# Three maxima and an all-partition reduction moved from the start of layer 1 to the end of layer 0, and two stores exchanged

## Chip, cores and metric

One core of one Trainium2 chip. The metric is the device time of one execution in microseconds (us). Of the kernel before there are three runs, and a profile of one further execution.

## The reference

Two graph-attention layers over the same 8192 nodes with 256 features; `adj` is a symmetric 0/1 matrix with about eight neighbours and the node itself in each row.

```python
h = maximum(layernorm(x), 0)                       # layer 0
Wh = h @ W
e  = (Wh @ a[:256])[:, None] + (Wh @ a[256:])[None, :]
x  = x + leaky_relu(softmax(where(adj == 0, -1e9, e)) @ Wh, 0.2)

h = maximum(layernorm(x), 0)                       # layer 1
h1, h2 = h @ a[:256], h @ a[256:]
e  = leaky_relu(h1 + h2.T, 0.01)
x  = x + softmax(where(adj > 0, e, -9e15)) @ h
```

## The kernel before, in words

Nodes are handled in T = 64 tiles of 128 rows. **Layer 0** is the first `nc.Block()`. For each tile the adjacency rows are loaded, converted, folded into 16-bit words and turned; TensorE multiplies the masks into the 64 value tiles (`aggregate`, L1016). VectorE (DVE) and ScalarE (ACT) then make the tile's new x (`normalise`, `add_x`, `copy_sums`), its new h (`finish`, L539), and the two products h1 and h2 (`dots`, L751), which `keep_dots` (L714 to L716) copies into `h1all`, `h2all` and the last column of `hh`; its three copies each raise `h12_kept`. SyncE (SP) stores x (`store_x1`, L372) and h (`store_h`, L377). The 46 tiles that come first also get a list of neighbours of each row; their rows are sorted by length, and the sorted records are written to memory by GpSimd (POOL), and loaded again by SP into `rec` (L400, semaphore `rec_in`).

At the end of layer 0 TensorE turns `h1all` (L1052), DVE copies the result out of PSUM (`h1T`, L968), and SP stores it as the h1 row (L404). SP then stores the last tile of h, and waits until all of its stores have landed (L405 to L412). The block's end is a barrier: no engine starts layer 1 before all have ended layer 0.

```python
sp.wait_ge(h1T_sb, 1)                               # L403
sp.dma_start(h1_d, h1T).then_inc(h1_out, 16)
store_h(T - 1, DENSE, NX - 1)
```

**Layer 1** is the second block, with two kinds of work side by side. The 18 remaining tiles are dense: TensorE multiplies masks (`adjp`, `adjn`) into two value arrays `Vp` and `Vn` (L1746), which are made in the first of six groups from tiles `hs` of h that SP loads; ACT makes the high halves (L1358) and DVE the low ones (L1521). The 46 sorted tiles are sparse: POOL gathers a row of h for each neighbour by indirect DMA (`gat`, L1334, 393 of them), ACT makes weights (L1390, L1398), DVE adds weighted rows (`sacc`, L1614 to L1636), and POOL scatters the 46 results (L1325). The gathers are made in batches of five or six rows with four buffers: before a batch is gathered, POOL waits until all rows of the batch four before it, whose buffer it takes, have been added (L1332, `row_added`); the first four batches hold 5, 6, 6 and 6 gathers, and the five batches behind them 5, 5, 5, 4 and 5; after the ninth (47 gathers) POOL scatters the first finished tile, and so on. SP holds six tiles' x for this work (L1229), and the load of the seventh waits for that first scatter; it stands in SP's program among the loads of `hs` (L1267), and those behind it wait with it. ACT and DVE issue dense and sparse work in an order written out by hand (`rows_by`, `prepare`, `add_rows`).

Before any of this, layer 1 takes the largest h2 of all nodes (it shifts the exponents), and two flags that say whether a list overflowed. DVE makes three maxima along the free axis into `red_in` (L1469, L1470, L1472; `exc` is L1468), POOL takes them over all partitions (L1321), and DVE goes on with `red` at L1476. POOL's first gather stands behind L1321 in its program, without needing its result:

```python
pool.wait_ge(mx_ready, 1)
nc.gpsimd.partition_all_reduce(red[:, :], red_in[:, :], P, RMAX).then_inc(M_all, 1)
```

SP begins layer 1 with loads: the h1 row to all partitions (L1212), four tiles of h (L1218), words of the adjacency (L1207), four more tiles (L1221).

Of the kernel before, what the change touches and what calls it, by code (L numbers as in the profile page):

```python
# [35 lines left out]
def two_layer_graph_attention(nc, x, adj, w0, a0, a1, key_pos, ident, tri, caps, row_ids, self_pos, out):  # L36
# [30 lines left out]
    P = 128  # L67
# [69 lines left out]
    with outer:  # L137
# [7 lines left out]
        cnt = outer.enter_context(nc.sbuf_tensor("cnt", [P, NS], f32))  # L145
        full = outer.enter_context(nc.sbuf_tensor("full", [P, 4], f32))
        idf = outer.enter_context(nc.sbuf_tensor("idf", [P, P], f32))


        ctx = ExitStack()  # L150
        with ctx:
            def sb(name, shape, dt):
                return ctx.enter_context(nc.sbuf_tensor(name, shape, dt))

            def sem(name):
                return ctx.enter_context(nc.semaphore(name))
# [145 lines left out]
            rank_ready = sem("rank_ready")  # L302
            rec_copied = sem("rec_copied")
            rec_in = sem("rec_in")
            h1T_ps = sem("h1T_ps")
            h1T_sb = sem("h1T_sb")
            h1_out = sem("h1_out")
# [17 lines left out]
            def _(sp):  # L325
# [49 lines left out]
                def store_h(t, off, b):  # L375
                    sp.wait_ge(h12_kept, 3 * t + 3)
                    sp.dma_start(h_rows(t + off), hh[:, b, :]).then_inc(hh_out[b], 16)  # L377

                def whole(t):

                    if t < T:
                        load(t, offset(t), range(0, 1), t == 0)
                    if PKL <= t < T + PKL:
                        store_words(t - PKL, offset(t - PKL), (t - PKL) % NPK)
                    if t < T:
                        load(t, offset(t), range(1, 2), t == 0)
                    if LAG <= t:
                        store_x1(t - LAG, offset(t - LAG), (t - LAG) % NX)
                    if XL <= t < T + XL:
                        load_x(t - XL, offset(t - XL), (t - XL) % NX, t - XL < NX)  # L390
                    if LAG + 1 <= t:
                        store_h(t - LAG - 1, offset(t - LAG - 1), (t - LAG - 1) % NX)
                    if t < T:
                        load(t, offset(t), range(2, Q), t == 0)
# [5 lines left out]
                sp.dma_start(rec_f[:, :, :], rec_d[:, 0:REC].rearrange("(m p) c -> p m c", p=P)).then_inc(rec_in, 16)  # L400
                for t in range(T + XL, T + LAG):
                    whole(t)
                sp.wait_ge(h1T_sb, 1)  # L403
                sp.dma_start(h1_d, h1T).then_inc(h1_out, 16)  # L404
                store_h(T - 1, DENSE, NX - 1)  # L405
                sp.wait_ge(rec_in, 16)
                sp.wait_ge(h1_out, 16)
                for b in range(NPK):
# [5 lines left out]
            @block.gpsimd  # L414
            def _(pool):

                nc.gpsimd.memset(eps[:, :], EPS).then_inc(ones_set, 1)
                nc.gpsimd.memset(hh[0:1, 0, 0:DV], 0.0).then_inc(dummy_set, 1)
                nc.gpsimd.memset(hh[0:1, 0, DV:ROW], NOTHING).then_inc(dummy_set, 1)
                nc.gpsimd.memset(HV[:, SH:T + SH, D:ROW], 1.0).then_inc(ones_set, 1)  # L420
                pool.wait_ge(dummy_out, 16)
                nc.gpsimd.memset(hh[:, :, D:DV], 1.0).then_inc(hh_ones, 1)
                pool.wait_ge(rmax_ready, 1)
                nc.gpsimd.partition_all_reduce(Mb[:, :], rmax[:, :], P, RMAX).then_inc(M_ready, 1)
                pool.wait_ge(rank_ready, 1)

                def copy_record(m):
                    nc.gpsimd.tensor_copy(xr[:, m % SH, 0:REC], rec_f[:, m, :]).then_inc(rec_copied, 1)

                def order(m):  # L430
                    pool.wait_ge(xs_in[m % SH], 16 * (m // SH + 1))
                    pool.wait_ge(rec_copied, m + 1)
                    pool.indirect_dma_start(rec_d, bass.IndirectOffsetOnAxis(ap=rank[:, m:m + 1], axis=0),
                                            xr[:, m % SH, :], None).then_inc(xs_out[m % SH], 16)

                for m in range(NS):
                    if m >= SH:
                        pool.wait_ge(xs_out[m % SH], 16 * (m // SH))
                    pool.wait_ge(x1_out[m % NX], 16 * (m // NX + 1))
                    pool.dma_start(xr[:, m % SH, REC:REC + D], x1_d[SP0 + m, :, :]).then_inc(xs_in[m % SH], 16)  # L440
                    copy_record(m)
                    if m >= 2:
                        order(m - 2)
                order(NS - 2)
                order(NS - 1)
                for i in range(SH):
                    pool.wait_ge(xs_out[i], 16 * len(range(i, NS, SH)))

            @block.scalar
            def _(act):  # L450
# [138 lines left out]
            def _(dve):  # L589
# [117 lines left out]
                def normalise(t, b):  # L707

                    dve.wait_ge(acc_ready, t + 1)
                    nc.vector.reciprocal(rden[:, b:b + 1], acc[b][:, D:DV]).then_inc(rden_ready, 1)  # L710

                def keep_dots(t, off, b):

                    nc.vector.tensor_copy(h1all[:, bass.ds(t + off, 1)], h12[:, 0:1]).then_inc(h12_kept, 1)  # L714
                    nc.vector.tensor_copy(h2all[:, bass.ds(t + off, 1)], h12[:, 1:2]).then_inc(h12_kept, 1)
                    nc.vector.tensor_copy(hh[:, b, DV:ROW], h12[:, 1:2]).then_inc(h12_kept, 1)  # L716
# [236 lines left out]
                for t in range(1, T):  # L953
                    step(t, t % UN, *counts(t), ahead=t + 1 < T, folds=t + 2 < T, listed=t + 2 < NS,
                         taken=t + 1 < NS, e=(t - 2) // UN if 2 <= t < NS + 2 else None)
                    if t == SORT:
                        sort_totals()
                    if t == SORT + 1:
                        sort_scan()
                    if t == SORT + 2:  # L960
                        sort_ranks()
                normalise(T - 1, 1)
                add_x(T - 1, NX - 1, *counts(T))
                scale_h(T - 1)
                dots(T - 1, NX - 1, counts(T)[2])
                keep_dots(T - 1, DENSE, NX - 1)
                dve.wait_ge(h1T_ps, 1)
                nc.vector.tensor_copy(h1T, kps[1][0:T, 0:P]).then_inc(h1T_sb, 1)  # L968

# [137 lines left out]
        with ctx:  # L1107
# [22 lines left out]
            tM = early[:, 6 * T:7 * T]  # L1130
            sS = early[:, 9 * T:9 * T + 2 * NS].rearrange("p (s t) -> p s t", s=2)
            tS = early[:, 11 * T:11 * T + NS]
            exc = sb("exc", [P, NS], f32)
            gat = sb("gat", [P, NBUF, BS, ROW], f32)
            sacc = sb("sacc", [P, NACC, 2, DV], f32)
            zself = sb("zself", [P, 2, NS], f32)
# [4 lines left out]
            hb = sb("hb", [P, 2, NS], f32)  # L1141
            srd = sb("srd", [P, 2], f32)
            M1 = sb("M1", [P, 4], f32)
            red_in = sb("red_in", [P, 3], f32)
            red = sb("red", [P, 3], f32)
            flag = sb("flag", [P, 1], f32)
            redi = sb("redi", [P, 1], i32)
            Es = sb("Es", [P, 2, T], f32)
# [8 lines left out]
            pkg_in = [sem(f"pkg_in{i}") for i in range(2)]  # L1157
            h1bc_in = [sem(f"h1bc_in{i}") for i in range(2)]
            x1g_in = sem("x1g_in")
            exc_ready = sem("exc_ready")  # L1160
            mx_ready = sem("mx_ready")
            M_all = sem("M_all")
            flag_ready = sem("flag_ready")
            redi_ready = sem("redi_ready")
            nh2_ready = sem("nh2_ready")
# [151 lines left out]

            @block.gpsimd
            def _(pool):
                pool.wait_ge(mx_ready, 1)  # L1320
                nc.gpsimd.partition_all_reduce(red[:, :], red_in[:, :], P, RMAX).then_inc(M_all, 1)  # L1321

                def scatter(m):
                    pool.wait_ge(so_ready, m + 1)
                    pool.indirect_dma_start(  # L1325
                        out, bass.IndirectOffsetOnAxis(ap=rec[:, m, OWN:OWN + 1], axis=0),
                        sout[:, m % NOUT, :], None).then_inc(so_out[m % NOUT], 16)

                done = 0
                for k, (m, s0, s1) in enumerate(batch):  # L1330
                    if k >= NBUF:
                        pool.wait_ge(row_added, begin[k - NBUF + 1])  # L1332
                    for s in range(s0, s1):
                        pool.indirect_dma_start(  # L1334
                            gat[:, k % NBUF, s - s0, :], None, h_d,
                            bass.IndirectOffsetOnAxis(ap=rec[:, m, s:s + 1], axis=0))\
                            .then_inc(gat_in[k % NBUF], 16)
                    while done < NS and last[done] + OUT_LAG <= k:
                        scatter(done)
                        done += 1  # L1340
                for m in range(done, NS):
                    scatter(m)
# [122 lines left out]
            def _(dve):  # L1465
                nc.vector.tensor_scalar(nh2[:, :], h2all[:, :], -BIG, None, ALU.mult)\
                    .then_inc(nh2_ready, 1)
                nc.vector.tensor_tensor(exc[:, :], rec_f[:, :, DEG], capv[:, :], ALU.subtract).then_inc(exc_ready, 1)  # L1468
                nc.vector.reduce_max(red_in[:, 0:1], h2all[:, :], AX.X)  # L1469
                nc.vector.reduce_max(red_in[:, 1:2], full[:, :], AX.X)  # L1470
                dve.wait_ge(exc_ready, 1)
                nc.vector.reduce_max(red_in[:, 2:3], exc[:, :], AX.X).then_inc(mx_ready, 1)  # L1472
                dve.wait_ge(M_all, 1)

                Mh = red[:, 0:1]
                nc.vector.tensor_scalar(M1[:, 2:3], Mh, -1.0, None, ALU.mult).then_inc(negM_ready, 1)  # L1476
# [319 lines left out]
```

## Time and profile before

| | |
|---|---|
| median of three runs | 1690.48 us |
| the three runs | 1688.31, 1690.48, 1691.74 us |
| the profiled execution | 1689.47 us |
| span from its first to its last instruction | 1687.3 us |
| mean granted TensorE clock | 0.973 |
| busy shares | PE 92%, DVE 74%, ACT 59%, POOL 33% |
| layer 1 | from 1069.1 us of the span to its end |

The profiled execution's own time is 2.2 us above its span; times in views are counted from the span's start. Busy shares average over two layers with different limits, so the views to read here are those of a stretch.

### The profile page before, as it was taken

How to read it: one execution, taken by the hardware profiler on the slowest of the kernel's cores; microseconds unless marked ns; L12 is line 12 of the kernel's file. 1: busy time of each engine (PE TensorE's matmuls, PEld its weight loads, DVE VectorE, ACT ScalarE, POOL GpSimd, SP SyncE). 2: the span in 40 equal slices, each digit the busy share in tenths (PEclk: the TensorE clock that was granted, in tenths of full speed). 3: DMA queues.
4: the chain of work that ended last, by engine and by line, in shares of the span. 5: the costliest groups of instructions: out<-in, count | busy, mean ns of one | idle time of the engine just before them, and what ended most of it. 6: DMA issues, size and time to landing. Idle time of an engine off the chain costs nothing. (4 is left out here: it accounts for less than half of the span.)

```text
span 1687.3 us, 37172 instructions
## 1 busy us (share of the span) xinstructions
PE 1551.5 (92%) x13443; PEld 1321.8 (78%) x13443; DVE 1255.9 (74%) x4759; ACT 989.5 (59%) x1514; POOL 562.5 (33%) x588
## 2 busy tenths in 40 slices
PE   6877999999999999999999999486898999989897
PEld 5645888888888888888888888365687877878786
DVE  6577998998898899887874453696866666666765
ACT  5978656665765566566666661675645445444542
POOL 0000000000000000000014554587777777777776
PEclk9998999999999999999999999798899999999999
DMA  9418989888988898898889994555444444444443
GB/s 318 172 43 341 348 303 364 320 301 313 369 310 300 329 358 310 301 374 319 331 337 385 393 361 112 178 132 153 119 135 114 130 123 129 115 142 117 128 113 107
DMA packets 141700, 406.91 MB, mean 241 GB/s; under 512 B 25857, under 2 KB 91586, under 8 KB 108834
## 3 DMA queue, kind: packets, MB, share of 16 engines
q1 hardware_dynamic: 116114, 335.11, 54.0%
q0 software_dynamic: 25488, 70.77, 14.7%
q8 instruction: 28, 0.46, 0.1%
q14 instruction: 70, 0.57, 0.1%
HBM read 365.39 MB, written 40.41 MB: 241 GB/s over the span
## 5 line engine op out<-in xcount | busy, mean ns | idle before, releaser
L1016 PE MATMUL banks<-HV,adjT 128*128 128x257 f16 x8192 | 938.8, 274 | 18.0 <-DVE adjT L673 10.2
L1016 PEld LDWEIGHTS banks<-HV,adjT 128*128 128x128 fp8e4 x8192 | 791.2, 97 | 150.8 <-DVE HV L703 23.8
L1746 PE MATMUL banks<-Vp,adjp 128*128 128x257 f16 x2304 | 451.9, 278 | 77.5 <-DVE adjp L1561 62.5
L458 ACT ACTIVATE adj_f<-adj_i 128x2048 fp8e4<-128x2048 int32 x256 | 480.1, 1898 | 5.6 <-DMA adj_i<-in_adj 5.5
L1334 POOL DMA_INDIRECT gat<-h_of_layer,rec x393 | 420.5, 1070 | 121.9 <-issue 115.3
L1746 PE MATMUL banks<-Vn,adjn 128*128 128x257 f16 x2304 | 451.0, 278 | 0.0
L1746 PEld LDWEIGHTS banks<-Vp,adjp 128*128 128x128 fp8e4 x2304 | 225.0, 99 | 121.7 <-issue 56.2
L440 POOL DMA_DIRECT2D xr<-x_after_layer x46 | 25.6, 557 | 834.4 <-DVE rank L941 772.5
L1746 PEld LDWEIGHTS banks<-Vn,adjn 128*128 128x128 fp8e4 x2304 | 227.1, 99 | 36.6
L1369 ACT ACTIVATE adjn<-h1bc,nh 128x384 fp8e5<-128x384 f32 x384 | 202.4, 604 | 0.0
L1390 ACT ACTIVATE e<-gat,hb 128x4 f32<-128x4 f32 (+3 forms) x168 | 41.2, 293 | 240.7 <-DMA gat<-h_of_layer,rec 240.5
L1620 DVE SCALAR_TENSOR_TENSOR sacc<-gat,w,sacc 128x257 f32<-128x257 f32 x347 | 157.4, 479 | 0.0
L1598 DVE TENSOR_TENSOR w<-e 128x5 f32<-128x5 f32 (+2 forms) x84 | 13.6, 162 | 165.7 <-ACT e L1390 165.5
L506 ACT ACTIVATE pk<-banks 128x512 uint16<-128x512 uint16 x64 | 37.7, 589 | 137.7 <-PE banks L1001 137.7
L670 DVE TENSOR_SCALAR adjT<-pk 128x512 uint16<-128x512 uint16 x448 | 94.8, 282 | 0.0
L710 DVE RECIPROCAL rden<-banks 128x1 f32<-128x1 f32 x64 | 10.7, 168 | 110.0 <-PE banks L1016 108.9
L989 PE MATMUL banks<-w_sb,hT 128*128 128x257 f32 x256 | 68.7, 392 | 15.9 <-ACT hT L470 15.6
L642 DVE SCALAR_TENSOR_TENSOR fold<-adj_f 128x1024 int32<-128x1024 int32 x64 | 77.3, 1207 | 7.7 <-ACT adj_f L458 7.6
L539 ACT ACTIVATE hh<-x,nmr,rstd 128x256 f32<-128x256 f32 x64 | 38.5, 601 | 60.8 <-DVE nmr L742 60.8
L533 ACT ACTIVATE std<-mv,eps 128x1 f32<-128x1 f32 x64 | 18.9, 295 | 92.8 <-DVE mv L734 92.5
L547 ACT ACTIVATE ysb<-banks,rden 128x256 f32<-128x256 f32 x64 | 29.8, 465 | 73.0 <-DVE rden L710 73.0
L751 DVE CUSTOM_DVE_ANT_0 junk<-hh,a1row 128x256 f32<-128x256 f32 x128 | 54.2, 423 | 11.9 <-ACT hh L539 9.7
(172 smaller groups left out, 1472.6 us busy)
## 6 DMA issues: line engine op xcount, KB each, us to landing
adj_i<-in_adj SPq DMA_DIRECT2D x256, 1024.0 KB, 7.2
h_of_layer<-hh SPq DMA_DIRECT2D x64, 129.0 KB, 6.6
hs<-h_of_layer SPq DMA_DIRECT2D x64, 129.0 KB
xt<-in_x SPq DMA_DIRECT2D x64, 128.0 KB, 7.0
packed_adj<-pk SPq DMA_DIRECT2D x64, 128.0 KB, 6.2
x_after_layer<-x SPq DMA_DIRECT2D x64, 128.0 KB, 7.0
HV<-in_x SPq DMA_DIRECT2D x14, 512.0 KB, 8.8
gat<-h_of_layer,rec POOLq DMA_INDIRECT x393
```

Of the source, the lines that this page charges most:

```text
L458: nc.scalar.activation(adj_f[:, b, q * QC:(q + 1) * QC], adj_i[:, q, :], ACT.Copy, scale=2.0, saturate=False).then_inc(conv_done, 1)
L539: nc.scalar.activation(hh[:, b, 0:D], x1[:, b, :], ACT.Relu, scale=rstd1[:, bass.ds(t, 1)], bias=nmr1[:, bass.ds(t, 1)]).then_inc(hh_ready, 1)
L642: nc.vector.scalar_tensor_tensor(four, whole[:, 0:4 * GW], 1, whole[:, 4 * GW:8 * GW], ALU.logical_shift_right, ALU.bitwise_or)\
L670: last = nc.vector.tensor_scalar(adjT[:, b, i, :], pk[:, pb, :], PAIR << i, 6 - i, ALU.bitwise_and, ALU.logical_shift_left)
L751: nc.vector.tensor_tensor_reduce(out=junk[:, :], in0=hh[:, b, 0:D], in1=a1row[:, s, :], scale=1.0, scalar=0.0, op0=ALU.mult, op1=ALU.add, ...
L989: last = nc.tensor.matmul(wps[t % 3][:, 0:DV], hT[:, t % 2, c, :], w_sb[:, c, :], start=(c == 0), stop=(c == 1))
L1016: last = nc.tensor.matmul(acc[b][:, 0:DV], adjT_h[:, b, i, q, :, h], V0[:, jb, s, 0:DV], start=(jb == 0 and s == 0), stop=(jb == T - 1 and ...
L1334: pool.indirect_dma_start(gat[:, k % NBUF, s - s0, :], None, h_d, bass.IndirectOffsetOnAxis(ap=rec[:, m, s:s + 1], axis=0))\
L1369: i = nc.scalar.activation(adjn_b[:, c % AN, jb // 2, :, jb % 2], h1bc[:, g2, :], ACT.Relu, scale=-BIG, bias=nh2[:, tiles[j]:tiles[j] + 1] ...
L1390: nc.scalar.activation(e8[:, k % 2, i, 0:s1 - s0], gat[:, k % NBUF, 0:s1 - s0, DV], ACT.Exp, scale=scale, bias=hb[:, i, m:m + 1]).then_inc ...
L1620: nc.vector.scalar_tensor_tensor(acc, x, w, acc, ALU.mult, ALU.add)\
L1746: mm = nc.tensor.matmul(bank[2 * i + part][:, 0:DV], m[:, i * P:(i + 1) * P], V[:, j, s, 0:DV], start=(j == 0 and s == 0), stop=(j == T - ...
```

## The change

The three maxima, `exc` and the reduction are taken out of layer 1 and put into layer 0. On DVE `exc` and two of the maxima stand ahead of the last tile's `normalise`, and the maximum of `h2all` stands between the last `keep_dots` and the copy of the h1 row, behind a wait for that `keep_dots`. On POOL the reduction stands at the end of its layer-0 program. The wait for its result on DVE goes: the barrier between the layers stands in its place. The tiles `exc`, `red_in` and `red` and three semaphores are allocated for both layers. On SP the last store of h is issued ahead of the h1 row's.

```diff
+        exc = outer.enter_context(nc.sbuf_tensor("exc", [P, NS], f32))
+        red_in = outer.enter_context(nc.sbuf_tensor("red_in", [P, 3], f32))
+        red = outer.enter_context(nc.sbuf_tensor("red", [P, 3], f32))
...
@@ layer 0, sync
                 for t in range(T + XL, T + LAG):
                     whole(t)
+                store_h(T - 1, DENSE, NX - 1)
                 sp.wait_ge(h1T_sb, 1)
                 sp.dma_start(h1_d, h1T).then_inc(h1_out, 16)
-                store_h(T - 1, DENSE, NX - 1)
                 sp.wait_ge(rec_in, 16)
@@ layer 0, gpsimd
                 for i in range(SH):
                     pool.wait_ge(xs_out[i], 16 * len(range(i, NS, SH)))
+                pool.wait_ge(mx_ready, 3)
+                nc.gpsimd.partition_all_reduce(red[:, :], red_in[:, :], P, RMAX).then_inc(M_all, 1)
@@ layer 0, vector
+                dve.wait_ge(rec_in, 16)
+                nc.vector.tensor_tensor(exc[:, :], rec_f[:, :, DEG], capv[:, :], ALU.subtract).then_inc(exc_ready, 1)
+                nc.vector.reduce_max(red_in[:, 1:2], full[:, :], AX.X).then_inc(mx_ready, 1)
+                dve.wait_ge(exc_ready, 1)
+                nc.vector.reduce_max(red_in[:, 2:3], exc[:, :], AX.X).then_inc(mx_ready, 1)
                 normalise(T - 1, 1)
                 add_x(T - 1, NX - 1, *counts(T))
                 scale_h(T - 1)
                 dots(T - 1, NX - 1, counts(T)[2])
                 keep_dots(T - 1, DENSE, NX - 1)
+                dve.wait_ge(h12_kept, 3 * T)
+                nc.vector.reduce_max(red_in[:, 0:1], h2all[:, :], AX.X).then_inc(mx_ready, 1)
                 dve.wait_ge(h1T_ps, 1)
                 nc.vector.tensor_copy(h1T, kps[1][0:T, 0:P]).then_inc(h1T_sb, 1)
@@ layer 1, gpsimd
-                pool.wait_ge(mx_ready, 1)
-                nc.gpsimd.partition_all_reduce(red[:, :], red_in[:, :], P, RMAX).then_inc(M_all, 1)
@@ layer 1, vector
                 nc.vector.tensor_scalar(nh2[:, :], h2all[:, :], -BIG, None, ALU.mult)\
                     .then_inc(nh2_ready, 1)
-                nc.vector.tensor_tensor(exc[:, :], rec_f[:, :, DEG], capv[:, :], ALU.subtract).then_inc(exc_ready, 1)
-                nc.vector.reduce_max(red_in[:, 0:1], h2all[:, :], AX.X)
-                nc.vector.reduce_max(red_in[:, 1:2], full[:, :], AX.X)
-                dve.wait_ge(exc_ready, 1)
-                nc.vector.reduce_max(red_in[:, 2:3], exc[:, :], AX.X).then_inc(mx_ready, 1)
-                dve.wait_ge(M_all, 1)
```

## Rows read from the trace of the kernel before

**Rows 1.** The page: chain that ended last by engine; the group of gathers (busy, mean ns | idle).

```profile
POOL 22%; issue 7%; DVE 3%; DMA 2%; ACT 1%; PE 0%; SPq 0%; DVEq 0%; ACTq 0%
...
L1334 POOL DMA_INDIRECT gat<-h_of_layer,rec x393 | 420.5, 1070 | 121.9 <-issue 115.3
```

**Rows 2.** Waits between 1083 and 1687 us: who for whom, us in total, times, longest.

```profile
POOL gat L1334 <- DVE sacc L1620: 6.6, 14, 2.6
```

**Rows 3.** Timeline of POOL in layer 1: start, length, engine, line [idle before, what ended it].

```profile
1106.19 2.22 POOL L1334 DMA_INDIRECT gat<-h_of_layer,rec  x1 [0.30 <-DVE sacc L1620]
...
1149.80 1.00 POOL L1325 DMA_INDIRECT out<-sout,rec  x1 [0.30 <-issue]
...
1164.80 0.94 POOL L1334 DMA_INDIRECT gat<-h_of_layer,rec  x1 [2.65 <-DVE sacc L1620]
```

**Rows 4.** Timeline of DVE: the first of its sparse rows, and the fourth to eighth.

```profile
1091.74 0.35 DVE L1614 TENSOR_SCALAR sacc<-gat,w 128x257 f32<-128x257 f32 x1
...
1097.71 2.07 DVE L1620 SCALAR_TENSOR_TENSOR sacc<-gat,w,sacc 128x257 f32<-128x257 f32 x5
```

**Rows 5.** Timeline of SP's queue between 1105 and 1160 us.

```profile
1105.10 20.02 SPq L1267 DMA_DIRECT2D hs<-h_of_layer  x13
1152.26 0.32 SPq L1229 DMA_DIRECT2D sout<-sorted_records  x1
```

**Rows 6.** The chain that ended last, 1140 to 1170 us: start, length, what.

```profile
1149.80 2.44 DMA out<-sout,rec
...
1154.10 4.50 DMA hs<-h_of_layer
```

**Rows 7.** Timeline of the end of layer 0, all engines.

```profile
1034.62 0.37 SPq L400 DMA_DIRECT2D rec<-sorted_records  x1
...
1060.16 0.17 DVE L710 RECIPROCAL rden<-banks 128x1 f32<-128x1 f32 x1 [9.44 <-PE banks L1016]
...
1065.19 0.14 DVE L716 COPY hh<-h 128x1 f32<-128x1 f32 x1
...
1065.73 0.28 DVE L968 COPY fold<-banks 64x128 f32<-64x128 f32 x1 [0.40 <-PE banks L1052]
1066.04 0.54 SPq L404 DMA_DIRECT2D h_row<-fold  x1
1066.63 0.58 SPq L377 DMA_DIRECT2D h_of_layer<-hh  x1
```

**Rows 8.** DMA issues between 1064.9 and 1069 us: KB each, us from issue to landing.

```profile
h_of_layer<-hh SPq DMA_DIRECT2D x1, 129.0 KB, 2.0
h_row<-fold SPq DMA_DIRECT2D x1, 32.0 KB, 1.8
```

**Rows 9.** DMA issues between 1015 and 1100 us: the load of the sorted records.

```profile
rec<-sorted_records SPq DMA_DIRECT2D x1, 713.0 KB, 6.8
```

**Rows 10.** Timeline of the first 7 us of layer 1, all engines.

```profile
1069.10 0.33 SPq L1212 DMA_DIRECT2D h1bc<-h_row  x1
...
1069.39 0.21 DVE L1469 TENSOR_REDUCE red_in<-h2all 128x1 f32<-128x64 f32 x1
...
1070.28 0.15 DVE L1476 TENSOR_SCALAR M<-red 128x1 f32<-128x1 f32 x1 [0.51 <-POOL red L1321]
...
1070.41 1.00 POOL L1334 DMA_INDIRECT gat<-h_of_layer,rec  x1 [0.16 <-issue]
...
1073.15 0.51 ACT L1358 ACTIVATE Vp<-hs,Es 128x258 f16<-128x258 f32 x1 [0.84 <-DMA hs<-h_of_layer]
...
1075.99 1.13 DVE L1539 TENSOR_SCALAR adjp<-pkg 128x384 uint16<-128x384 uint16 x4 [2.88 <-DMA pkg<-packed_adj]
```

**Rows 11.** POOL's gathers (L1334) by stretch: length, POOL busy (count), clock, DMA share, GB/s.

```profile
1109.00:1149.00 40.00, 33.30 (x23) 0.91 0.42 114
1149.00:1189.00 40.00, 27.36 (x25) 0.83 0.62 179
...
1269.00:1669.00 400.00, 272.13 (x268) 0.98 0.44 123
```

More of the change, by code:

```diff
@@ L304, in two_layer_graph_attention @@
             rec_in = sem("rec_in")
+            exc_ready = sem("exc_ready")
+            mx_ready = sem("mx_ready")
+            M_all = sem("M_all")
             h1T_ps = sem("h1T_ps")
@@ L1132, in two_layer_graph_attention @@
             tS = early[:, 11 * T:11 * T + NS]
-            exc = sb("exc", [P, NS], f32)
             gat = sb("gat", [P, NBUF, BS, ROW], f32)
@@ L1143, in two_layer_graph_attention @@
             M1 = sb("M1", [P, 4], f32)
-            red_in = sb("red_in", [P, 3], f32)
-            red = sb("red", [P, 3], f32)
             flag = sb("flag", [P, 1], f32)
@@ L1159, in two_layer_graph_attention @@
             x1g_in = sem("x1g_in")
-            exc_ready = sem("exc_ready")
-            mx_ready = sem("mx_ready")
-            M_all = sem("M_all")
             flag_ready = sem("flag_ready")
```

## The prediction

> **What bounds the kernel now.** Start with the page's chain that ended last [rows 1]. POOL's own work holds 22% of the span and "issue" 7%: 29% of 1687.3 us is 489 us, nearly all of it in layer 1 (618 us). The row of the gathers says why: 393 gathers of 1070 ns, and of the 121.9 us that POOL stood idle before them, 115.3 are the 0.3 us that it needs between two. POOL gathers almost without a stop, and layer 1 is about as long as its gathers.
>
> Next, the waits: does anything ever hold POOL? DVE is named 14 times, 6.6 us in all, the longest 2.6 [rows 2]. Read such a row with the timeline. At the twenty-fourth gather, 1106.19, the idle time is 0.30 us and DVE is named [rows 3], but 0.30 is POOL's usual gap, and what it needs there is five rows added by DVE. DVE began its first at 1091.74, and had eight by 1099.8 [rows 4]. POOL did not wait: the rows were there some 7 us before. Without the usual gaps the 14 waits come to 6.6 - 14 x 0.3 = 2.4 us, and the one at 1164.80 holds them all.
>
> That one belongs to POOL too, by a detour through SP. SP issued loads of h until 1125.1, and the next thing in its queue came at 1152.26 [rows 5]. It was held by a result tile that POOL had yet to scatter, at 1149.80 [rows 3]. From there the chain goes through the scatter's transfer, SP, and the next tiles of h [rows 6] to ACT, DVE, and POOL at 1164.80. So dense and sparse work alike hang on how soon POOL has done its first 47 gathers and that scatter. Time that POOL wins at its first gather is time won at the end; time won by the other engines at the start of layer 1 is not.
>
> **The exchange of the two stores.** In layer 0 the last DVE copy of h ended at 1065.33; the h1 row was stored at 1066.04, h at 1066.63 [rows 7]. From issue to landing they took 1.8 and 2.0 us [rows 8]: the row landed at 1067.84, h at 1068.63, and layer 1 began at 1069.10 [rows 10], 0.47 us behind it. With the change h is issued at about 1065.36 and lands at 1067.36; its issue is over (0.58 us) by 1065.94, ahead of the row's, at 1066.04 as before. The last to land is then the row, at 1067.84, and layer 1 begins at 1068.31: **0.8 us gained**. Bounds: no such order is in the trace; with h's 2.0 us plus 0.2 of queueing behind it the gain is 0.4, with a landing 0.1 sooner 0.9. I take 0.8, as h is four times the row's size and still landed in 2.0.
>
> **The early maxima.** `exc` and two maxima (0.21 us is the longest maximum [rows 10]; three such pieces, some 0.65 us) now stand ahead of the last tile's reciprocal, where DVE sat idle for 9.44 us waiting for TensorE [rows 7]: nothing; uncovered, 0.65 us. The wait that they bring is for the sorted records: issued at 1034.62 [rows 7], 6.8 us to land [rows 9], so there at 1041.4, while DVE comes to it when that idle time begins, at 1050.7. Nothing either.
>
> **The last maximum.** It waits for the copies that end at 1065.33, and takes 0.21 us [rows 10]: over by 1065.57. Queued behind it on DVE is the copy of the h1 row, for which SP waits, and for SP everyone. That copy had 0.40 us of idle time before it, until TensorE's result at 1065.73 [rows 7]: the maximum fits in with 0.16 us to spare. Nothing; at worst, if it fell behind that result, 0.2 us lost.
>
> **The reduction on POOL.** The maxima ended at 1069.77 and DVE's next instruction began at 1070.28, 0.51 us later [rows 10]. In its new place that is 1065.57 to 1066.08, while SP waits for its stores until 1067.84: hidden, with 1.8 us to spare. Behind it on POOL there is only the barrier.
>
> **POOL's earlier start.** Its first gather was issued at 1070.41, 1.31 us after SP's first load [rows 10], as it stood behind the reduction. Now nothing stands ahead of it. With its usual gap of 0.30 us from the barrier's end (0.06 us ahead of SP's first load) it is issued 0.24 us after that load: **1.07 us gained** beyond the barrier. Bounds: at once would be 1.3; with 0.5 us more for a first instruction, 0.6. I take 1.07, by the gap of which the 115.3 us of idle time are made.
>
> The lead is 0.85 of a gather at the clean pace of 0.95 + 0.30 us (0.94 at 1164.80 [rows 3]). From 1109 to 1149 the pace was 40 / 23 = 1.74 us [rows 11], and there 0.85 of a gather is worth 1.5 us; the gathers just ahead of the scatter are clean ones again, so I keep 1.07. The Trainium skill (SBUF — State Buffer, "SBUF: two separate sides") says that a DVE instruction which takes the port pair shared with GpSimd locks GpSimd out of writing descriptors until it ends. By it the slow stretch belongs to DVE's work and not to POOL's count, and a lead kept all through it would make the gain 0.8 + 1.5 = 2.3 instead of 1.9.
>
> **What leaves layer 1.** DVE has the reduced maximum about 1.05 us sooner (1070.28 against 1069.2 of the old times). I cost this at nothing: ACT then still waits 0.84 us for tiles of h at 1073.15, and DVE 2.88 us for adjacency words at 1075.99 [rows 10], loads that SP starts at the barrier. Those are late next; and DVE and ACT have the 7 us in hand that were found above. The same slack covers what the earlier gathers take from these loads: at most their lead, 1.07 us.
>
> **The sum.** 0.8 + 1.07 = 1.9 us gained, kept by POOL to the scatter and, through SP, to the end. Bounds: 0.4 + 0.6 - 0.2 = 0.8, and 0.9 + 1.3 = 2.2, or 2.3 as above. The profiled execution took 1689.47, which leaves 1687.6; it lies 1.0 us below the median of the three runs, 1690.48, and from that the sum gives **1688.6 us**. A measurement of this kernel can tell about 0.2%, 3.4 us, from no change; the three runs alone lie 3.4 us apart.
>
> **Rivals.**
> *Only the barrier counts.* If DVE's rows or the tiles of h hold POOL after all, the maxima's move is lost and the stores' exchange is left, less what the gathers take from the loads (0.2 of their 1.07): 0.6 us, 1689.9. For it: the wait at 1164.80, and DVE named in 14. Against it: five rows were there 7 us before they were wanted, and SP stood for 27 us on POOL's scatter.
> *Nothing arrives.* The row lands late behind h, and POOL's first gather is held up by something at the layer's start that the reduction hid: 1690.5.
> *Longer gathers (slower).* A gather isn't always 0.95 us: the one at 1106.19 took 2.22 [rows 3]. From 1109 to 1189, 48 gathers took 60.7 us; at the late mean, 272.1 / 268 = 1.015, they would have taken 48.7, so 12 us were lost there [rows 11]. The change moves POOL against DVE by about 1 us, and which gathers are held may come out otherwise. Half as much again, 6 us, gives 1690.5 - 1.9 + 6 = 1694.6. It decides from the point where those 48 gathers take over 66 us (60.7 + 1.9 + 3.4). The lock named above is this mechanism in general; no row here shows it by itself.
> *Shorter gathers.* The same with a third less lost, 4 us: 1684.6.
> *The change doesn't do what it says.* The reduction might still be waited for, in layer 0: if POOL's took over 1.8 us there, the barrier would be later instead. The 0.51 us above speaks against it; its price is under the barrier's gain, and I give it nothing of its own.
>
> **How the numbers follow.** The forecast, 1688.6, has 0.62; only the barrier 0.15; nothing 0.07; longer gathers 0.06; shorter gathers 0.10. Each is blurred by the runs' spread of 1.7 us on either side. Faster by over 0.2% is below 1687.1: all of "shorter gathers", a sixth of the forecast and a little of its neighbour, 0.21. Slower, above 1693.9: most of "longer gathers", 0.05. Within: 0.74. For the range, the forecast's upper bound of the gain with the spread is 1690.5 - 2.3 - 1.7 = 1686.5, stretched to 1686.0 for part of the shorter gathers; "only the barrier" with its spread is 1691.6. Outside lie some 2 in 10.
>
> **What would show it.** Right: after TensorE's last layer-0 matmul SP's first load of layer 1 comes 0.8 us sooner, POOL's first gather 1.9 us sooner, POOL's first scatter and the wait at its end of the detour about 1.9 us sooner too; DVE waits longer than 2.88 us for its words. Wrong: the h1 row lands over 2.2 us after its issue; DVE's copy of it starts later behind TensorE's transpose; POOL's first gather comes over 0.8 us after SP's first load; POOL waits by more than its 0.3 us at the twenty-fourth gather; or the 48 gathers from the twenty-sixth take 4 us more or less than 60.7.

## The result, and the profile after

The changed kernel takes 1695.89 us in the median of eight runs (1693.69 to 1697.56); the kernel before, in eight runs beside it, 1690.13. The ratio is 1.0032 (95% interval 1.0022 to 1.0042): **slower by some 5.4 us**, where 1.9 us less was forecast and 1691.6 was the top of the range. The profiled execution took 1696.78, with a span of 1694.6 us against 1687.3.

Begin at the end of layer 0, in the timeline of all engines after; these rows answer to [rows 7] and [rows 10].

```profile
1065.03 0.22 DVE L981 TENSOR_REDUCE red_in<-h2all 128x1 f32<-128x64 f32 x1
1065.38 0.28 DVE L983 COPY fold<-banks 64x128 f32<-64x128 f32 x1
1065.46 0.38 POOL L455 PARTITION_ALL_REDUCE red<-red_in  x1 [33.53 <-DVE red_in L981]
1065.69 0.54 SPq L411 DMA_DIRECT2D h_row<-fold  x1
1073.68 1.28 ACT L1353 ACT_TABLE_LOAD   x1 [9.93 <-PEq L154]
1073.69 0.34 SPq L1221 DMA_DIRECT2D h1bc<-h_row  x1
...
1074.38 1.01 POOL L1340 DMA_INDIRECT gat<-h_of_layer,rec  x1 [8.54 <-POOLq L154]
...
1078.31 0.51 ACT L1364 ACTIVATE Vp<-hs,Es 128x258 f16<-128x258 f32 x1 [2.55 <-DMA hs<-h_of_layer]
```

Up to 1065.69 all is as planned: the last maximum fits in ahead of the copy, POOL reduces at once, the h1 row goes out. Then no engine runs an instruction for 8.0 us. From the issue of the row to SP's first load of layer 1 it was 1069.10 - 1066.04 = 3.06 us before; it is now 1073.69 - 1065.69 = 8.00. Layer 1 begins 4.9 us later after the row, and POOL's first gather says whom it waited for: line 154, the block's own line, on POOL's queue. The view of that line lists what the sequencers, which issue each engine's instructions, did there (count, shortest/median/longest in ns, start).

```profile
L154 POOLq EVENT_SEMAPHORE  x2: 17/17/17, 1073.5 to 1073.6; - x2
...
L154 DVEq DRAIN  x1: 322/322/322, 1065.4 to 1065.4; - x1
L154 POOLq DRAIN  x1: 8027/8027/8027, 1065.4 to 1065.4; - x1
...
L154 SPq DRAIN  x1: 7/7/7, 1067.8 to 1067.8; - x1
```

SP was through at 1067.8, where it was expected. POOL was not: each engine ends the block with a drain, and POOL's takes 8.0 us where DVE's takes 0.3. The barrier's semaphores follow it at once. The same view of the kernel before, in which this line is 151:

```profile
L151 POOLq DRAIN  x1: 7578/7578/7578, 1034.8 to 1034.8; - x1
...
L151 SPq DRAIN  x1: 7/7/7, 1068.9 to 1068.9; - x1
```

It was always there. POOL was done with layer 0 at 1034.8, drained until 1042.4, and that cost nothing, as the barrier waited for SP until 1068.9. The change gives POOL an instruction that can't start before 1065.4, and with it the drain moves: 1065.84, the reduction's end, plus 7.6 is 1073.4.

Behind it the two traces run side by side. The scatter that came at 1149.80 and the wait that ended at 1164.80 [rows 3] are in POOL's timeline after:

```profile
1154.29 1.00 POOL L1331 DMA_INDIRECT out<-sout,rec  x1 [0.30 <-issue]
...
1168.88 0.95 POOL L1340 DMA_INDIRECT gat<-h_of_layer,rec  x1 [1.96 <-DVE sacc L1620]
```

4.5 and 4.1 us late, as layer 1's start was by 4.6 on the span's clock. The gathers by stretch, 4.6 us shifted, answer to [rows 11]: from 1113.6 the same 33.30 us for 23 gathers, then 28.04 for 27.36.

```profile
1113.60:1153.60 40.00, 33.30 (x23) 0.91 0.42 115
1153.60:1193.60 40.00, 28.04 (x25) 0.83 0.61 179
```

So the rival of longer gathers didn't decide this. The rest of the profiled difference (7.3 us at the end of the span, against 4.1 here) gathers in small steps over the next 500 us. It isn't a steady part of the loss: in the second trace of the changed kernel, below, POOL's last scatter came 4.8 us later than before the change, and in this one 7.3.

### The profile page after: what moved, and what is told of

It reads as the page before. It is cut to its first block and busy times, and to the rows that moved or that the text cites. A ratio compares the mean times of both kernels' runs of the same rounds, so it can differ in the third digit from the quotient of the medians.

```text
span 1694.6 us, 37171 instructions
## 1 busy us (share of the span) xinstructions
PE 1550.8 (92%) x13443; PEld 1322.5 (78%) x13443; DVE 1256.2 (74%) x4759; ACT 989.1 (58%) x1514; POOL 569.2 (34%) x588
## 5 line engine op out<-in xcount | busy, mean ns | idle before, releaser
L1340 POOL DMA_INDIRECT gat<-h_of_layer,rec x393 | 426.8, 1086 | 129.7 <-issue 115.8
```

The lines of the kernel that those rows point to most:

```text
L1340: pool.indirect_dma_start(gat[:, k % NBUF, s - s0, :], None, h_d, bass.IndirectOffsetOnAxis(ap=rec[:, m, s:s + 1], axis=0))\
```

## The experiments

Theory D: the loss is POOL's drain at the end of the block. Rival R: the reduction itself takes long when it stands there. Rival G: the cost is in gathers that meet other DVE work. Each ratio is to the kernel before in runs on the same chip (29 to 35 of it, 11 or 12 of each experiment). Its medians there were 1688.39, 1687.43 and 1691.43 us, and in the first such set it alone ran from 1682.0 to 1692.3 us; the intervals reach 1.5 to 2.8 us to either side, so a smaller difference is read from the traces and not from the time.

**The wait alone.** To the kernel before, only this is added at the end of POOL's layer-0 program:

```diff
                 for i in range(SH):
                     pool.wait_ge(xs_out[i], 16 * len(range(i, NS, SH)))
+                pool.wait_ge(h12_kept, 3 * T)
```

> The kernel before with one wait added at the end of GpSimd's layer-0 program, for the last copies of the dots (h12_kept at its full count); no reduction, no maxima and no store is moved. Theory D: GpSimd's drain starts at about 1065.3 and ends 7.6 to 8 us later, at 1073; layer 1 begins about 4 us later than before, and the time is 1694 to 1695. Rival R: there is no late reduction, so nothing changes: 1690. Rival G: 1690 too.

1691.10 us, ratio 1.0016 (1.0002 to 1.0029): 2.7 us, where 4 to 5 were expected. The view of the block's line, and SP's timeline:

```profile
L151 POOLq DRAIN  x1: 7578/7578/7578, 1067.0 to 1067.0; - x1
...
L151 SPq DRAIN  x1: 7/7/7, 1070.2 to 1070.2; - x1
```

```profile
1067.42 0.54 SPq L404 DMA_DIRECT2D h_row<-fold  x1
...
1074.83 0.33 SPq L1213 DMA_DIRECT2D h1bc<-h_row  x1
```

No instruction was moved; the drain now starts when the wait is over and lasts the same 7578 ns, and layer 1 begins 7.41 us after the row, 4.35 later than before. 4.35 us is 1.0026, inside the interval. The time only just excludes no change at all; the trace shows the delay itself. R is out as the cause: there was no late reduction, and SP was through at 1070.2.

**A wait that ends early.** The same place, an earlier event:

```diff
+                pool.wait_ge(x1_ready, T - 1)
```

> The kernel before with a wait at the end of GpSimd's layer-0 program for an earlier event: x of the tile before the last (x1_ready at T - 1), some 14 us ahead of the last x. Theory D: GpSimd's drain starts at about 1047.5 us and ends at 1055, still 13 us ahead of the barrier, so layer 1 begins 3.0 us after the issue of the h1 row as before and the ratio is 1.000. Rival W (any wait, or any drain that starts late in layer 0, costs time, wherever it ends): 1.0016 again.

1688.49 us, ratio 1.0005 (0.9994 to 1.0017).

```profile
L151 POOLq DRAIN  x1: 7578/7578/7578, 1049.1 to 1049.1; - x1
```

```profile
1067.43 0.54 SPq L404 DMA_DIRECT2D h_row<-fold  x1
...
1070.50 0.33 SPq L1213 DMA_DIRECT2D h1bc<-h_row  x1
```

The drain ends at 1056.7, and layer 1 begins 3.07 us after the row, as before. The 1.0016 of rival W lies just inside the interval, so the time alone doesn't exclude it; the barrier, which did not move, does. A late drain costs only by what of it lies beyond SP's last landing.

**The changed kernel again**, without an edit, on the same chip as the early wait.

> The changed kernel once more, beside the kernel before on another chip, to set its loss against that of the added wait (1.0016, 1.0002 to 1.0029). Theory D (GpSimd's drain at the block's end is all of the loss): layer 1 begins 7.4 to 8 us after the copy of the h1 row and the ratio is 1.002 to 1.0035, that is 4.6 us late, less or more the noise. Rival G (the moved work costs something of its own, in gathers): the drain's share is about 1.0025 and the ratio lies clear above it, 1.004 or more.

1692.83 us, ratio 1.0027 (1.0015 to 1.0039): 4.6 us, with 7.99 us from the row to layer 1.

```profile
1065.62 0.54 SPq L411 DMA_DIRECT2D h_row<-fold  x1
1073.61 0.34 SPq L1221 DMA_DIRECT2D h1bc<-h_row  x1
```

The drain's delay is all that is needed. The interval ends just short of the 1.004 or more of rival G; the versions without the late reduction, below, settle that.

**The stores alone.** In the kernel before, the exchange of the two stores and nothing else.

```diff
+                store_h(T - 1, DENSE, NX - 1)
                 sp.wait_ge(h1T_sb, 1)
                 sp.dma_start(h1_d, h1T).then_inc(h1_out, 16)
-                store_h(T - 1, DENSE, NX - 1)
```

> The kernel before with the exchange of the two stores alone. Theory D (the loss is GpSimd's drain at the end of the block, which takes about 8 us and starts only when GpSimd has passed its last wait): GpSimd's drain still starts at about 1034.8 us and is hidden, layer 1 begins about 0.8 us sooner after the copy of the h1 row (3.0 us before, 2.3 here), and the time is up to 0.8 us below the kernel before: 1689.3. Rival R (the late reduction itself takes some 8 us to end, which its row of 0.38 us does not show): the same here. Rival G (the loss is in gathers that meet other VectorE work): nothing certain, within 3 us on either side.

> The kernel before with the exchange of the two stores alone, once more (0.9995, 0.9983 to 1.0006 before). Theory C: layer 1 begins 0.75 us sooner after the h1 row, as does the first gather, so 0.9996. Rival G: 1.000 or above.

Ratios 0.9995 (0.9983 to 1.0006) and 1.0003 (0.9991 to 1.0015). The trace of the first has what was worked out, 2.31 us from the row to layer 1 for 3.06, so 0.75 us gained; the time can't tell 0.75 us from nothing.

```profile
1067.25 0.54 SPq L405 DMA_DIRECT2D h_row<-fold  x1
1069.56 0.34 SPq L1212 DMA_DIRECT2D h1bc<-h_row  x1
```

**All of the change but the reduction's place.** The maxima stay in layer 0; the reduction is POOL's first instruction of layer 1. Against the changed kernel:

```diff
@@ layer 0, gpsimd
-                pool.wait_ge(mx_ready, 3)
-                nc.gpsimd.partition_all_reduce(red[:, :], red_in[:, :], P, RMAX).then_inc(M_all, 1)
@@ layer 1, gpsimd
+                pool.wait_ge(mx_ready, 3)
+                nc.gpsimd.partition_all_reduce(red[:, :], red_in[:, :], P, RMAX).then_inc(M_all, 1)
@@ layer 1, vector, ahead of the first use
+                dve.wait_ge(M_all, 1)
```

> The changed kernel with the reduction put back as GpSimd's first instruction of layer 1; the maxima stay in layer 0, the stores stay exchanged. Theory D: the drain is hidden again (it starts at about 1034.8), layer 1 begins 0.8 us sooner than in the kernel before, the first gather about 0.5 us sooner still, and the time is 1689 (0 to 1.5 us below before). Rival R: the same, since the reduction was followed by a gather after 0.16 us there. Rival G: the loss of 5.8 us stays for the most part, as the maxima and the stores are still moved: 1694 or more.

> The changed kernel with the reduction as GpSimd's first instruction of layer 1, once more (0.9994, 0.9977 to 1.0010 before). Theory C (time at GpSimd's first gather arrives at the end): its first gather comes 1.3 us sooner after the h1 row than in the kernel before, so 0.9992. Rival G (the gain is lost in the gathers that follow): 1.000 or above.

The third has three tiles more, that nobody uses:

```diff
+        ones3 = outer.enter_context(nc.sbuf_tensor("ones3", [P, P], f32))
+        top3 = outer.enter_context(nc.sbuf_tensor("top3", [P, 1], f32))
+        dg3 = outer.enter_context(nc.sbuf_tensor("dg3", [P, 4], f32))
```

> The same kernel with the three tiles allocated that the reduction on TensorE used, and nothing done with them: all that changes is where the tiles lie in SBUF, by some 532 bytes in each partition. Theory M (the place of the tiles is why the reduction on TensorE measured 1.0012 twice, though its first gather came 1.4 us sooner): 1.001 or more, and clear of the kernel without the tiles. Otherwise the same as that one, 0.9992.

Ratios 0.9994 (0.9977 to 1.0010), 0.9995 (0.9986 to 1.0004) and, with three unused tiles, 0.9990 (0.9977 to 1.0003). No interval excludes 1, so a gain isn't shown, but all three lie about the 0.9992 that the traces give: the first gather comes 3.07 us after the row's issue instead of 4.37, 1.3 us sooner. In the timeline of the second:

```profile
1067.01 0.54 SPq L411 DMA_DIRECT2D h_row<-fold  x1
1069.32 0.34 SPq L1219 DMA_DIRECT2D h1bc<-h_row  x1
1069.39 0.40 POOL L1328 PARTITION_ALL_REDUCE red<-red_in  x1 [36.17 <-POOLq L154]
1070.08 1.01 POOL L1341 DMA_INDIRECT gat<-h_of_layer,rec  x1 [0.29 <-issue]
```

All three intervals end at 1.0010 or below, and those of the changed kernel begin at 1.0015 or above. The same maxima, the same stores, one instruction on the other side of the barrier: that is the whole loss, and the moved maxima and stores have no part in it. This is the version to keep, if any; where the tiles lie made no difference that can be seen.

**The reduction without POOL.** TensorE turns the maxima, DVE takes the three largest and sets them on a diagonal, TensorE spreads them with a matmul by ones. Against the changed kernel, with the allocation of three tiles, a memset and some waits left out:

```diff
@@ layer 0, gpsimd: the wait and the reduction are left out
...
@@ layer 0, tensor, at the end
+                pe.wait_ge(mx_ready, 3)
+                nc.tensor.transpose(kps[0][0:3, 0:P], red_in[:, :], idf[:, :]).then_inc(h1T_ps, 1)
+                pe.wait_ge(exc_ready, 3)
...
+                nc.tensor.matmul(kps[0][:, P:P + 3], ones3[0:3, :], dg3[0:3, 0:3], start=True, stop=True)\
+                    .then_inc(h1T_ps, 1)
...
@@ layer 0, vector, behind the copy of h1T
...
+                nc.vector.reduce_max(top3[0:3, :], kps[0][0:3, 0:P], AX.X).then_inc(exc_ready, 1)
...
+                nc.vector.tensor_scalar(dg3[0:3, 0:3], idf[0:3, 0:3], top3[0:3, 0:1], None, ALU.mult).then_inc(exc_ready, 1)
...
+                nc.vector.tensor_copy(red[:, :], kps[0][:, P:P + 3]).then_inc(M_all, 1)
```

> The changed kernel with the reduction over partitions made without GpSimd: TensorE transposes the three columns of maxima, VectorE takes their maxima and puts them on a diagonal, TensorE spreads them over all partitions with a matmul by ones, VectorE copies them out, all at the end of layer 0. Nothing is left on GpSimd there. Theory D: the drain is hidden, layer 1 begins at most 0.8 us sooner than before (0.3 if the chain of five small steps outlasts the landing of the h1 row), the first gather comes 1.2 to 1.9 us sooner than before, and the time is 1688 to 1689.5. Rival R: the same. Rival G: the loss of 5.8 us stays for the most part, 1694 or more.

> The kernel with the reduction on TensorE once more. It measured 1.0012 (1.0000 to 1.0025), though its trace has the drain hidden, layer 1 begun 0.7 us sooner after the h1 row and the first gather 1.4 us sooner. Theory D: that was the spread of the runs, and the ratio is now 0.999 to 1.0005. Rival G: what is gained at the start is lost again in the gathers, and it is 1.001 or more once more.

Ratios 1.0012 (1.0000 to 1.0025) and 1.0012 (0.9999 to 1.0026): a miss. In both traces the drain is hidden and layer 1 begins 2.32 us after the row; the first gather comes 3.00 us after it, 1.4 sooner than before. In the timeline of the first:

```profile
1066.97 0.54 SPq L414 DMA_DIRECT2D h_row<-fold  x1
1069.29 0.34 SPq L1235 DMA_DIRECT2D h1bc<-h_row  x1
1069.97 0.99 POOL L1354 DMA_INDIRECT gat<-h_of_layer,rec  x1 [35.80 <-POOLq L157]
```

By theory C of the expectations above (time at POOL's first gather arrives at the end) it should have come out like the version before it, about 0.999. The unused tiles alone don't explain it. What takes the time back wasn't found, and the two traces can't show it: both profiled executions (1686.33 and 1684.82 us) are the fastest of their twelve, and their spans are shorter than that of the kernel before.

**What a delay of the first gather costs.** The kernel before, with ten more reductions that nobody needs between POOL's reduction and its first gather.

```diff
+            spare = sb("spare", [P, 10, 3], f32)
...
                 nc.gpsimd.partition_all_reduce(red[:, :], red_in[:, :], P, RMAX).then_inc(M_all, 1)
+                for i in range(10):
+                    nc.gpsimd.partition_all_reduce(spare[:, i, :], red_in[:, :], P, RMAX)
```

> The kernel before with ten more reductions of the same kind, into a spare tile that nobody reads, between GpSimd's reduction in layer 1 and its first gather; nothing else moves. By the spacing of such instructions (0.54 us) the first gather comes some 5.4 us later. Theory C (the prediction's: time at the first gather is time at the end): the whole delay arrives, 1.0032. Rival L (VectorE and the waits behind it pace the first 47 gathers, so that a lead or a delay of GpSimd is taken up there): half of it or less, 1.0016 or below.

```profile
1066.35 0.54 SPq L404 DMA_DIRECT2D h_row<-fold  x1
...
1070.46 3.58 POOL L1324 PARTITION_ALL_REDUCE spare<-red_in  x10
1074.20 1.01 POOL L1337 DMA_INDIRECT gat<-h_of_layer,rec  x1 [0.16 <-issue]
```

The delay was smaller than meant, as the ten took 0.36 us each: the first gather comes 7.85 us after the row for 4.37, 3.5 us later. 1691.83 us, ratio 1.0029 (1.0017 to 1.0040), that is 2.9 to 6.7 us. The whole 3.5 us (1.0021) fits, half of it (1.0010) doesn't: in the median of the runs a delay of POOL alone, with nothing else moved, arrives at the end. The trace doesn't show it: the profiled execution, 1687.29 us, is the fastest of the twelve, and in it the first scatter comes at 1148.70, 74.5 us after the first gather, where the kernel before had it at 1149.80 after 79.4.

## Why the prediction was wrong

**The step that failed** is "The reduction on POOL": it was to be hidden, "with 1.8 us to spare", as "behind it on POOL there is only the barrier". The reduction took the 0.4 us that its row gave. But between POOL's last instruction and the barrier stands a drain of 7.6 us, and it starts only when POOL's last wait is over. With 1065.84 + 7.6 in place of 1066.08 POOL is through at 1073.4 in the changed kernel and the barrier comes at 1073.5, not at 1068. Counted from the row's issue, layer 1 begins 4.9 us later instead of 0.8 sooner, and POOL's first gather comes 1074.38 - 1065.69 = 8.7 us after the row for 4.4 before: 4.3 us lost, 1.0026, which both measurements of the change hold (1.0022 to 1.0042, 1.0015 to 1.0039). The term was to be had beforehand: the rows of the block's line in the trace before held 7578 ns for POOL, hidden by 27 us of idle time. I read the durations of what moves, and not what it pushes along. One rival had the place ("if POOL's took over 1.8 us there, the barrier would be later instead") and got no chance of its own. Nor did one of the five signs of being wrong come: the row landed 1.8 us after its issue, and the first gather came 0.69 us after SP's first load. They watch the row, DVE's copy and the gathers, and none of them the barrier.

**The exchange of the stores** was right: 0.75 us in the trace, 0.79 worked out. So were the covers: the early maxima and the last one delayed nothing (TensorE's turn of `h1all` ended at 1065.35, the copy of the h1 row began at 1065.38), and SP was through at 1067.8.

**POOL's earlier start** was mis-sized. Where nothing stands ahead of the first gather (the reduction on TensorE) it comes 0.68 us after SP's first load, not 0.24; the gain beyond the barrier is 0.63 us, near the lower bound of 0.6, and not 1.07. A reduction ahead of it costs almost nothing (0.76 us after that load): it starts at 0.07 us, at a time when the gather hadn't begun without it either.

**POOL bounds layer 1** was right in what it said of a delay: the wait at the twenty-fourth gather was none, the scatter and the wait behind it moved by layer 1's delay, and 3.5 us on POOL alone arrived in the runs' median. Its reverse, that a lead arrives too, is shown only weakly: three versions with a lead of 1.3 us lie at 0.9990 to 0.9995, one with 1.4 at 1.0012.

**The spread** was taken too small: 1.7 us to either side, from three runs, where 35 runs of the kernel before on one chip lie within 10.3 us. That isn't why the forecast failed, but it is far more than the 1.9 us that were to be measured. Part of it may lie in the gathers. From its first gather to its 58th instruction (gathers and scatters) POOL needed 94.4 us in the trace before, 94.5 after, 90.0 with the stores exchanged and 89.2 with the late gathers; two traces of one kernel differ by 0.3 us (the changed one) to 2.1 (the reduction in layer 1). What makes a gather long no run here separates.

## What to carry to other kernels

Work that is moved in front of a barrier moves the end of its engine's program, and with it everything that the engine does between its last instruction and the barrier. Look up the drain of each engine in the trace (here 7.6 us on POOL, 0.3 on DVE) before giving an engine that has been done for long one more late instruction, or even one more wait. On the far side of the barrier the same instruction cost next to nothing here.

## What the runs showed of the hardware that was not expected

POOL's drain at the end of layer 0 takes 7578 ns, to the nanosecond, in the eleven traces in which POOL came to it with all its waits over or with a wait alone, and 8027 and 8023 ns where a reduction of 0.38 us was still to run. It doesn't depend on how long POOL has stood idle: it started at 1034.8, 1049.1 and 1067.0 us with the same length. A first gather right behind the barrier comes 0.68 us after SP's first load, while a reduction in the same place comes after 0.07 (1069.39 against 1069.32).

The same drain stands at the end of layer 1, and there nothing hides it. In the kernel before, the view of the second block's line, with POOL's last scatter ahead of it:

```profile
1678.29 0.96 POOL L1325 DMA_INDIRECT out<-sout,rec  x1 [0.30 <-issue]
...
L1107 POOLq DRAIN  x1: 9216/9216/9216, 1677.8 to 1677.8; - x1
...
L1107 SPq DRAIN  x1: 72/72/72, 1685.2 to 1685.2; - x1
```

SP, whose last stores had landed, came to its own drain at 1685.2. POOL's, which here holds the last scatter, ended at 1687.0, 7.8 us after that scatter's end, and the span ended at 1687.3. In all thirteen traces POOL's drain (9207 to 9231 ns) ends last, 1.6 to 2.0 us after SP came to its own. So the kernel's end hangs on POOL's last instruction too, with this drain behind it. That ending POOL's work sooner there would bring up to some 1.8 us is an estimate from these rows; no run tried it.
